# A selective-scan layer on one core: scan inputs in four PSUM banks and two units ahead, the y sums by channel block in two banks, C broadcast later in its queue, the u transposes moved

## The reference, cut to what matters

```
h  = layernorm(x) * (1 + ca) + sa
xz = h @ w_in.T + b_in ;  x_ssm, z = split(xz) ;  z = silu(z)
dt = softplus(x_ssm @ w_dt.T + b_dt) ;  B = x_ssm @ w_B.T + b_B ;  C = x_ssm @ w_C.T + b_C
for every t:  s = exp(A * dt) * s + dt * B * x_ssm       # s is [512, 16]
              y = sum over n of s * C
y  = (y + D * x_ssm) * z ;  pre = y @ w_out.T + b_out + h
x  = x + ga * (layernorm(pre) * gamma + beta)
x  = x + gb * ffn(layernorm(x) * (1 + cb) + sb)          # 64 small networks of 16 relus
```

## Time and profile before

| | |
|---|---|
| median of 3 runs | 4935.87 us (4935.53 to 4944.75) |
| the profiled execution's own time | 4929.93 us |
| its span, first to last instruction | 4928.2 us |
| mean granted TensorE clock | 0.935 of 2.4 GHz |
| instructions | 58251 |

### The profile page before, as it was taken

The page is one execution under the profiler, slowest core; times in us unless marked ns, Lnnn a source line. Parts: engine busy times, 40 slices in busy tenths (PEclk is TensorE's granted clock), DMA queues, the critical chain, the costliest instruction groups (busy, mean ns, idle before and its releaser), DMA issues. The chain is left out here.

```text
span 4928.2 us, 58251 instructions
## 1 busy us (share of the span) xinstructions
PE 4129.9 (84%) x18432; PEld 2434.8 (49%) x18432; DVE 3630.0 (74%) x4620; ACT 3819.0 (77%) x6371; POOL 3516.3 (71%) x1775
## 2 busy tenths in 40 slices
PE   7888888888888888888888888888888888888877
PEld 3544545545455445455454554454554445544544
DVE  4877777777777777777777777777777777777775
ACT  4778778778787787787787777887877877778875
POOL 2777677776677776777777777767777767777674
PEclk8999999999999999999999999999999999999988
DMA  4666555665565665555765556655657555566554
GB/s 137 148 150 139 139 135 135 141 155 139 133 144 135 156 138 138 138 133 140 158 141 140 139 131 152 148 138 133 139 136 166 132 136 138 132 151 148 137 128 103
DMA packets 200747, 690.13 MB, mean 140 GB/s; under 512 B 25254, under 2 KB 25254, under 8 KB 147195
## 3 DMA queue, kind: packets, MB, share of 16 engines
q0 software_dynamic: 59904, 436.23, 43.3%
q1 hardware_dynamic: 140538, 250.19, 16.9%
HBM read 215.50 MB, written 34.63 MB: 51 GB/s over the span
## 5 line engine op out<-in xcount | busy, mean ns | idle before, releaser
L378 POOL TENSOR_TENSOR work<-work,c_bc 128x2048 f32<-128x2048 f32 x448 | 2040.8, 4555 | 737.2 <-DVE state L1169 476.5
L1161 DVE TENSOR_TENSOR_SCAN work<-work,state,b_ps 128x512 f32<-128x512 f32 x1792 | 2245.9, 1272 | 414.8 <-PE b_ps L493 403.5
L493 PEld LDWEIGHTS b_ps<-ident,work 128*128 128x128 f32 x8192 | 1022.0, 147 | 1328.3 <-issue 625.5
L493 PE MATMUL b_ps<-ident,work 128*128 128x128 f32 x8192 | 1307.5, 284 | 412.1 <-DVE work L1161 399.4
L876 ACT ACTIVATE work<-u_td,b_td 128x512 f32<-128x512 f32 x2048 | 1457.2, 712 | 122.6 <-PE b_ps L493 117.0
L866 ACT ACTIVATE work<-dt_t,neg_a 128x512 f32<-128x512 f32 x2048 | 1457.8, 712 | 84.7 <-DMA work<-work 83.7
L711 PE MATMUL dense<-h_t,w_in_t 128*128 128x512 f32 x1024 | 568.9, 657 | 7.4 <-DVE u_td L1244 7.3
L648 PE MATMUL dense<-h_t,w_in_t 128*128 128x512 f32 x1024 | 543.5, 643 | 3.8 <-ACT h_t L880 3.6
L619 PE MATMUL dense<-w_out_t,proj 128*128 128x512 f32 x1024 | 542.2, 630 | 0.0
L493 PE MATMUL dense<-ident,xn 128*128 128x128 f32 x1536 | 261.3, 298 | 325.5 <-POOL xn L442 208.3
L677 PE MATMUL dense<-xs_t,w_dt_t 128*128 128x512 f32 x1024 | 503.3, 595 | 0.0
(11 more groups left out here) (116 smaller groups left out, 4909.0 us busy)
## 6 DMA issues: line engine op xcount, KB each, us to landing
work<-work POOLq DMA_DIRECT2D x384, 1024.0 KB, 8.1
c_bc<-c_d SPq DMA_DIRECT2D x512, 256.0 KB, 3.4
xn<-in_x SPq DMA_DIRECT2D x128, 256.0 KB, 4.6
work<-xs_t POOLq DMA_DIRECT2D x32, 1024.0 KB, 7.7
x<-in_x SPq DMA_DIRECT2D x128, 256.0 KB, 4.5
out_dram<-x SPq DMA_DIRECT2D x128, 256.0 KB, 5.8
work<-in_wmod SPq DMA_DIRECT2D x2, 1024.0 KB, 6.6
w_in_t<-in_w_in_t SPq DMA_DIRECT2D x2, 1024.0 KB, 10.0
```

The costliest lines, as they stand in the source:

```text
L378: gp.tensor_tensor(out, states, c_of(s, n).rearrange("p (a t) -> p a t", a=1).to_broadcast([P, KD, T]), ALU.mult).then_inc(S["prod_done"], 1)
L493: return nc.tensor.transpose(dst, src, ident[:, :])
L1161: V.tensor_tensor_scan(ring[:, i % RING, :], ring[:, i % RING, :], b_ps[:, i % 2, :], state[:, i:i + 1] if s % NC else 0.0, ALU.mult, ALU. ...
```

## The change

It has five parts.

1. `b_ps` has four banks in place of two. PE turns the input of unit i + 2 at unit i (`LEAD`), and waits for scan x - 4 in place of x - 2. `y_ps` gets two banks in place of four.
2. The y sums are no longer made set by set at two places, but by channel block: `add_sets(b, j)` at unit j = 0 to 3 of the next step, 16 transposes each, all four sets, in bank j % 2. DVE copies block j at unit j + 1. `turn_y` and the gate's multiplication use the two banks in turn.
3. State n = 14 gets a wide product in place in `ring` (one of 128x2048 in place of four of 128x512); PE reads it there, so the decays of the next chunk's units 8 to 11 wait for these sums. `acc` keeps three sets, each always in the same slot.
4. `spread_c` stands three units later in SP's queue, for the same n.
5. In `ORDER`, `s` comes before `z.2`, and the four u transposes lie in `z.2` and `z.3`: PE issues ut.0 to ut.3 at units 57, 59, 60, 62 (before: 54, 56, 58, 59), DVE takes them at 58, 60, 61, 62 (before: 55, 56, 58, 60). The gate part `z.2` is done at unit 59 (before: 57), so POOL's third gate moves from unit 61 to 63. `GROUPS` and the waits of PE follow.

```diff
-    WIDE = N - 2
-    CHAIN = WIDE // 2 - 1
-    SETS = 4
+    B_RING, LEAD, Y_RING = 4, 2, 2
+    Y_AT = 0
+    WIDE, CHAINED = N - 1, N - 2
+    CHAIN = CHAINED // 2 - 1
+    SETS, KEPT = 4, 3
...
-        z.2.0 ut.0 z.2.1 z.2.2 ut.1 z.2.3
-        s.0 ut.2 s.1 s.2 ut.3 s.3
-        z.3.0 z.3.1 z.3.2 z.3.3""".split()
+        s.0 s.1 s.2 s.3
+        z.2.0 z.2.1 ut.0 z.2.2 z.2.3 ut.1
+        z.3.0 ut.2 z.3.1 z.3.2 ut.3 z.3.3""".split()
...
         return (k * KEPT + which) % ACC_RING
...
+        at_set = k * KEPT + which - ACC_RING
+        return at_set // KEPT, (KD - 1) * SETS + (1, 2, 4)[at_set % KEPT]
...
-                    if i % KD == 0:
+                    if i % KD == KD - 1:
                         n = i // KD + 2
                         if n < N and has_s:
                             spread_c(s, n)
...
-                pe.wait_ge(S["scan_done"], at("scan_done", s, i - 1))
+                pe.wait_ge(S["scan_done"], at("scan_done", s, i + 1 - B_RING))
...
+            def add_sets(b, j):
+                at_bank = j % Y_RING
+                if j >= Y_RING:
+                    pe.wait_ge(S["y_copied"], at("y_copied", b, j + 1 - Y_RING))
                 else:
+                    pe.wait_ge(S["yzt_done"], at("yzt_done", b - 1, KD - Y_RING + j + 1))
+                for which in range(SETS):
+                    if which == 0:
+                        pe.wait_ge(chain_done[0], chain_landed(b, CHAINED - 2))
+                    elif which == 1:
+                        pe.wait_ge(chain_done[1], chain_landed(b, CHAINED - 1))
+                    else:
+                        pe.wait_ge(S["prod_done"], at("prod_done", b, products(CHAINED + which - 2, j)))
+                    src = (ring[:, CHAINED * KD % RING + j, :] if which == 2
+                           else acc[:, set_slot(b, min(which, KEPT - 1)), j, :])
+                    for tb in range(TB):
+                        last = mm(y_ps[:, at_bank, tb * P:(tb + 1) * P], src[:, tb * P:(tb + 1) * P], ident[:, :],
+                                  is_transpose=True, start=(which == 0 and tb == 0), stop=(which == SETS - 1 and tb == TB - 1))
+                    last.then_inc(S["y_added"], 1)
...
                 for i in range(U):
-                    if has_s and i + 1 < U:
-                        turn_v(s, i + 1)
+                    if has_s and i + LEAD < U:
+                        turn_v(s, i + LEAD)
                     beside.until(i)
-                    if has_f and i + 1 == U:
-                        turn_v(f, 0)
-                    if has_b and i < 3:
-                        for which, j in (((1, 0), (1, 1), (1, 2), (1, 3)), ((3, 0), (3, 1)), ((3, 2), (3, 3)))[i]:
-                            add_set(b, which, j)
-                    if has_s and i >= U - 4:
-                        for j in ((0, 1), (2, 3))[i % 2]:
-                            add_set(s, 0 if i < U - 2 else 2, j)
+                    if has_f and i == U - 1:
+                        for n in range(LEAD):
+                            turn_v(f, n)
+                    if has_b and Y_AT <= i < Y_AT + KD:
+                        add_sets(b, i - Y_AT)
...
-                if r // KD < 2 or r // KD >= WIDE:
+                if r // KD == CHAINED:
+                    act.wait_ge(S["y_added"], at("y_added", k, j * SETS + 3))
+                elif r // KD < 2 or r // KD >= WIDE:
...
-                    yield 3 + tb // 3
+                for j in range(KD):
+                    yield Y_AT + j + 1
...
+                    dve.wait_ge(S["y_added"], at("y_added", b, (j + 1) * SETS))
```

More of the change, by code:

```diff
@@ L74, in set_slot @@
     def set_slot(k, which):
-        return (k * SETS + which) % ACC_RING
+        return (k * KEPT + which) % ACC_RING
     def set_freed(k, which):
-        at_set = k * SETS + which - ACC_RING
-        return at_set // SETS, (0, 2, 1, 3)[at_set % SETS] * KD + KD
+        at_set = k * KEPT + which - ACC_RING
+        return at_set // KEPT, (KD - 1) * SETS + (1, 2, 4)[at_set % KEPT]
     def slot(*part):
@@ L384, in unit_product @@
                     wait_for_c(s, n)
-                    freed = set_freed(s, n - WIDE + 2)
+                    freed = set_freed(s, KEPT - 1)
                     gp.wait_ge(S["y_added"], at("y_added", *freed))
                 gp.wait_ge(S["scan_done"], at("scan_done", s, i + 1))
-                gp.tensor_tensor(acc[:, set_slot(s, n - WIDE + 2), j, :], ring[:, i % RING, :], c_of(s, n), ALU.mult
+                gp.tensor_tensor(acc[:, set_slot(s, KEPT - 1), j, :], ring[:, i % RING, :], c_of(s, n), ALU.mult
                                  ).then_inc(S["prod_done"], 1)
@@ L472, in step @@
                     if has_s:
-                        if i % KD == 1 and 2 <= n < WIDE:
+                        if i % KD == 1 and 2 <= n < CHAINED:
                             add_to_chain(s, n)
@@ L552, in turn_v @@
                     pe.wait_ge(S["v_done"], at("v_done", s, (n + 1) * TB))
-                pe.wait_ge(S["scan_done"], at("scan_done", s, i - 1))
+                pe.wait_ge(S["scan_done"], at("scan_done", s, i + 1 - B_RING))
                 for tb in range(TB):
-                    last = turn(b_ps[:, i % 2, tb * P:(tb + 1) * P], v[:, n % V_RING, tb, j * P:(j + 1) * P])
+                    last = turn(b_ps[:, i % B_RING, tb * P:(tb + 1) * P], v[:, n % V_RING, tb, j * P:(j + 1) * P])
                 last.then_inc(S["b_made"], 1)
[L558 to L565, removed]
-                else:
[L567 to L572, removed]
@@ new lines, in add_sets @@
+            def add_sets(b, j):
+                at_bank = j % Y_RING
+                if j >= Y_RING:
+                    pe.wait_ge(S["y_copied"], at("y_copied", b, j + 1 - Y_RING))
+                else:
+                    pe.wait_ge(S["yzt_done"], at("yzt_done", b - 1, KD - Y_RING + j + 1))
[6 more added lines that the diff above has]
+                        pe.wait_ge(S["prod_done"], at("prod_done", b, products(CHAINED + which - 2, j)))
+                    if which == 2:
+                        src = ring[:, CHAINED * KD % RING + j, :]
+                    else:
+                        src = acc[:, set_slot(b, min(which, KEPT - 1)), j, :]
+                    for tb in range(TB):
+                        last = mm(y_ps[:, at_bank, tb * P:(tb + 1) * P], src[:, tb * P:(tb + 1) * P], ident[:, :],
+                                  is_transpose=True,
+                                  start=(which == 0 and tb == 0), stop=(which == SETS - 1 and tb == TB - 1))
+                    last.then_inc(S["y_added"], 1)
@@ L805, in dense @@
                         turn_b(s, f)
+                if has_b:
+                    for k in range(KD):
+                        yield slot("s", k)
+                        add_s(s, f, b, k)
                 for k in range(KD):
@@ L809, in dense @@
                         add_z(s, f, b, 2, k)
-                    if has_f and k in (0, 2):
+                    if has_f and k in (1, 3):
                         yield slot("ut", k // 2)
@@ L819, in dense @@
                         turn_u(s, f, 2 + k // 2)
[L820 to L823, removed]
             def step(s, has_s, has_f, has_b, has_c):
@@ L1187, in take_y @@
             def take_y(s, b, c):
-                for tb in range(TB):
-                    yield 3 + tb // 3
[L1190 to L1193, removed]
+                for j in range(KD):
+                    yield Y_AT + j + 1
+                    if j == 0:
+                        dve.wait_ge(S["dec_done"], at("dec_done", b, U))
+                        dve.wait_ge(S["u_done"], at("u_done", b, KD))
+                    dve.wait_ge(S["y_added"], at("y_added", b, (j + 1) * SETS))
+                    V.tensor_copy(y_sb[:, b % 2, :, j * P:(j + 1) * P],
+                                  y_ps[:, j % Y_RING, :].rearrange("p (b d) -> p b d", b=TB)).then_inc(S["y_copied"], 1)
                 for j in range(KD):
```

45 lines of the change are left out of this document (22 added, 23 removed).

## The result

The changed kernel takes 4763.75 us (median of 4 runs, 4755.83 to 4768.6) against 4936.26 for the kernel before: a ratio of 0.9645 with a 95% interval of 0.9628 to 0.9663. It is 172.5 us faster, 3.5%, where 391 us (7.9%) were forecast. The time lies near the slow end of the stated range (4420 to 4780), past rival A's 4738, and 44% of the forecast gain came, so the sum was wrong.

The account below looks back on a forecast made before the run. No engine is full; a ring of waits between engines bounds the step. Savings of 6.7 (part 4), 1.5 (part 1) and 4.5 (parts 2 and 5), 12.7 us over 31 steps, less a 4 us tail, gave 4545 us, range 4420 to 4780.

Parts of the forecast that it names:

- rival A: Only SP's queue helps, 5 to 8 us a step through `x1`, while parts 2 and 5 cancel: 4738 us, chance 0.22.
- What was to be late next: Before DVE's last `x1` moments: POOL's wide product of n = 5 delays the last addition, 5.8 us, about even with DVE's work.
- 8 gained: Step's end, part 5: later u transposes shorten the stretch from POOL's last u to the next first scan, 8 us.
- 3.5 given back: Chunk border, part 2: y sums between scan inputs lose 3 us, ACT's third relu waiting for POOL's gate about 1.
- The length of the new chain: From POOL's last u to the next first scan: some 14 us, decided by DVE, against 22.1 in the old order.
- the step that was called tight: Step's end: ut.3 at unit 62, copy, `v` and transposes take about 2 us, with 2.7 us of DVE work as cover.
- The clock: PE's matmuls after the 5.95 us wait: half clock costs 1.3 to 2 us each time, counted inside part 4's 6.7.
- B: More than forecast: rest of the stall, freed clock and more of 14.9 us input waits, 17 us a step: 4413, chance 0.17.
- C: No change: ACT, busiest beside PE, sets the pace and its 119.2 us a step stay: 4936 us, chance 0.03.
- D: Slower: PE stops at unit 0's y sums for the chain's DMA and POOL's products, DVE starves: 5026 us, chance 0.08.
- a sign of being wrong: DVE's copies of y waiting over 3 us a step for PE would show the forecast wrong.
- signs of being right: DVE's `x1` wait under 70 us, PE's for POOL's u under 2 a step, step about 137, clock above 0.95.

Follow-up runs that it names:

- c_only: The kernel before with part 4 alone (C broadcast three units later in SP's queue): 4691.9 us, ratio 0.9512.
- lead1: The changed kernel with PE turning scan inputs one unit ahead in place of two, still in four banks: 4598.7 us, ratio 0.9324.
- ring2_norm: ring2 with the first norm of the next chunk three units earlier on DVE and ACT: 4567.4 us, ratio 0.9268.
- ring2: The changed kernel with two banks for scan inputs and one unit of lead, as before the change: 4556.8 us, ratio 0.9239.
- c_ut: The kernel before with parts 4 and 5 alone (C later, s before z.2, u transposes later): 4511.9 us, ratio 0.9141.

## Why the forecast was wrong: part 1, and two sizes that cancelled

In the order in which the runs add the parts, the gain splits into -241 (part 4), -180 (part 5), -4 (part 3), +49 (part 2), +42 (two more banks) and +165 (the second unit of lead), together -169 us; measured -172.5. Since each is the distance to the run before it, the sum has to come out and proves nothing; and in another order the sizes would differ, as part 4's 241 and 194 do.

- **Part 4, 6.7 us a step forecast.** Measured 7.2 in units 21 to 27, 6.7 in 5 to 27 together, 7.8 over the step. What was to be late next, POOL's product of n = 5 ahead of the last sum, fits what DVE still waits for in `c_only`: 58.4 / 31 = 1.9 us a step, where 2.0 was left.
- **Parts 2 and 5, 4.5 us a step together.** Measured (180 - 49) / 31 = 4.2. The parts of this sum were both too large: 8 gained was 5.8, 3.5 given back was 1.6. That their difference came out is luck. The length of the new chain was right: from POOL's last u (ready at 2357.02) to the next first scan (2371.20) the changed kernel needs 14.2 us, where 14 were worked out; where the missing 2 us of the gain went is open. In the step that was called tight, ut.3 to the first scan, ACT waits for the copies (177.2 us in all).
- **Part 3, nothing.** Measured 4 us within the intervals of both.
- **Part 1, 1.5 us a step gained, with 0 as the lower bound: this is the step that failed.** It cost 207 us, 6.7 us a step: 165 by the second unit of lead and 42 by the two banks. The text had the reason in its hand and priced it at zero: "Another cost is that `v` is needed a unit earlier, and ACT is full from 2401 on, so I take no gain there." ACT makes `v` at a fixed unit of its own order, and that order was left as it was, so PE's earlier question brings `v` no earlier. What counts is then not what is gained but what stands behind PE's new wait, and it was the xs matmuls that ACT itself needs. The working looked at the banks' dependence (scan x - 4 in place of x - 2), which can only loosen, and not at the dependence on `v`, which the lead tightens.
- **The clock.** It was left out of the sum as part of the stall. It belongs in the other column as well: the three waits on PE shown here (2.92 us in the changed kernel, 3.89 in `lead1`, 3.54 in `ring2_norm`) were each followed by work at the half clock. The windows of 6 us around the same matmuls behind xn (after the stretch and its length: busy us and instructions of PE, PEld, DVE, ACT and POOL, the granted clock, the share of the DMA engines that was busy, GB/s) have `lead1` at 0.72 and `ring2` at 1.00:

```profile
2346.00:2352.00 6.00, 6.00 (x17) 3.10 (x16) 2.56 (x4) 5.36 (x10) 5.92 (x3) 0.72 1.00 216
```

```profile
2327.00:2333.00 6.00, 5.63 (x23) 2.85 (x21) 4.05 (x7) 5.55 (x11) 5.92 (x3) 1.00 1.01 211
```

  PE's timelines show what led there. `lead1`:

```profile
2344.74 0.66 PE L495 MATMUL dense<-ident,xn 128*128 128x128 f32 x4 [3.89 <-ACT xn L944]
...
2345.67 3.21 PE L629 MATMUL dense<-w_out_t,proj 128*128 128x512 f32 x4
```

  `ring2`:

```profile
2319.22 0.66 PE L495 MATMUL b_ps<-ident,work 128*128 128x128 f32 x4 [1.53 <-DVE work L1169]
...
2325.92 0.66 PE L495 MATMUL dense<-ident,xn 128*128 128x128 f32 x4 [2.15 <-ACT xn L944]
...
2326.85 1.88 PE L629 MATMUL dense<-w_out_t,proj 128*128 128x512 f32 x4
```

  With four banks PE goes straight to the transposes of xn and stands there 3.89 us in one piece; with two it stands 1.53 us for a scan first and then 2.15 us, and the four matmuls behind take 1.88 us in place of 3.21. Over the span PE's wait for xn is 119.4 us with four banks and 62.6 with two. That the 42 us between the two kernels went away with the xn wait speaks for this as the reason why looser banks cost. It covers 1.0 us of the 1.6 a step (units 5 to 27: 51.6 against 50.6, and 49.7 against 49.6 with the earlier norm); the other 0.6, behind unit 41, was not looked into. What the clock alone is worth was not separated from the wait.
- **Rivals.** A gave 4738, nearest to the measured 4764, but by another mechanism: parts 2 and 5 don't cancel (they give 131 us), it is part 1 that takes. B's term, more of the 14.9 us a step of waits for inputs, did come (461.9 us fell to 206.2), and was paid for by PE's waits for `v`. C: ACT, busiest by occupancy beside PE, keeps its busy time (3819.0 and 3815.3 us), and 8.6% was still to be had in `c_ut`. The Trainium skill ("Perfetto Trace Analysis", Identifying the Most-Contended Engine) says to optimize the engine of highest occupancy first. This case doesn't bear it out: ACT had nothing taken off, and shorter waits paid. D: PE didn't stop for the chain's DMA (its waits in front of the y sums are under 1 us in all), but DVE's in-order copies did wait, 225.2 us, or 7.3 a step. That was over the 3 us a step that the prediction named as a sign of being wrong, but it isn't what failed: `ring2` has 223.1 us of the same wait. Of the signs of being right, the waits came (52.2 us for `x1`, 16.4 of PE for POOL's u, both over the span) and so did the clock (0.962); the step took 145.0 us in place of 137. No sign looked at PE's wait for `v`.

## What to carry to other kernels

When a producer is moved ahead in a queue, look at each of its inputs, not only at the buffer that was the reason: the buffer wait gets looser and the input wait tighter, and what stands behind it in the queue pays. A command queue that mixes transfers on different clocks (broadcasts paced by one engine, loads by another) is worth a look before anything with more code: one line, without an instruction more, was the larger part of what this change could give. Test the parts of a joint change one by one; here two of the five made 421 us and the other three, added to them, gave 252 back.

## What the runs showed of the hardware that I had not expected

- Removing a dependency can slow a kernel: with two more banks and nothing else changed, 4556.8 us became 4598.7, and the traces show one long PE wait (3.89 us) in place of two short ones (1.53 and 2.15).
- A PE wait of 2.15 us (`ring2`, in front of xn) left the clock full: the next four matmuls take 1.88 us. In the kernel before, a wait of 2.08 us at the same place was followed by four matmuls in 3.48 us, with the granted clock at 0.50 from 2363 to 2366:

```profile
2361.84 0.65 PE L493 MATMUL dense<-ident,xn 128*128 128x128 f32 x4 [2.08 <-ACT xn L936]
...
2362.86 3.48 PE L619 MATMUL dense<-w_out_t,proj 128*128 128x512 f32 x4
```

  The length of the wait alone doesn't decide, and no run here shows what does.
- Between the two kernels the median time to landing of x's stores fell from 5.8 to 3.9 us and that of its loads rose from 4.5 to 6.2 us, with sizes unchanged, as part 6 of the page after shows:

```profile
x<-in_x SPq DMA_DIRECT2D x128, 256.0 KB, 6.2
out_dram<-x SPq DMA_DIRECT2D x128, 256.0 KB, 3.9
```
